# A layer of linear attention in four rounds: the next round's features are made within the heads, and the second norm is spread over the next round

## What is computed

```python
q, k, v = src @ Wq + bq, src @ Wk + bk, src @ Wv + bv      # 16 heads of 64
Q = jax.nn.elu(q) + 1.0
K = jax.nn.elu(k) + 1.0
KV = jnp.einsum('bshd,bshm->bhdm', K, v)
Z = 1.0 / (jnp.einsum('bshd,bhd->bsh', Q, K.sum(axis=1)) + EPS)
o = jnp.einsum('bshd,bhdm,bsh->bshm', Q, KV, Z).reshape(b, s, H * DH)
x = _layer_norm(src + o @ Wo + bo, g1, be1)
y = gelu(x @ W1 + b1) @ W2 + b2
return _layer_norm(x + y, g2, be2)                          # added to x by the caller
```

## Time and profile before

| | us |
|---|---|
| median of 3 runs | 3260.01 (3257.52 to 3273.21) |
| profiled execution, its own time | 3263.29 |
| its span, first to last instruction | 3261.6 |
| mean granted TensorE clock | 0.934 |
| TensorE matmuls busy | 2924.0 (90%) |
| VectorE / ScalarE / GpSimd busy | 1800.6 (55%) / 1350.9 (41%) / 683.8 (21%) |

### The profile page before, as it was taken

How to read it: one execution, slowest core, us unless ns; L and a number is a source line. 1 busy time by engine, 2 the same in 40 slices (tenths; PEclk the granted TensorE clock), 3 DMA queues, 4 the chain that set the end, 5 groups by cost and what they waited for, 6 DMA issues and landing times.

```text
span 3261.6 us, 64530 instructions
## 1 busy us (share of the span) xinstructions
PE 2924.0 (90%) x24081; PEld 1889.0 (58%) x24081; DVE 1800.6 (55%) x5820; ACT 1350.9 (41%) x3669; POOL 683.8 (21%) x1535
## 2 busy tenths in 40 slices
PE   8999988787799996998778997659999999999899
PEld 7888856555457774666445775444444444444465
DVE  6777765656326666756866665762233233333444
ACT  4565552223238882236676885421112111121221
POOL 3444420000017770003304663000000000000000
PEclk9999998988899996987788998979999999999999
DMA  5111100000012110030022113012000000000000
GB/s 129 46 49 46 47 24 1 1 1 1 4 27 53 47 31 22 1 108 4 13 45 59 39 40 136 2 53 76 1 1 1 1 1 1 1 1 1 1 1 14
DMA packets 158813, 91.86 MB, mean 28 GB/s; under 512 B 74211, under 2 KB 155750, under 8 KB 157414
## 3 DMA queue, kind: packets, MB, share of 16 engines
q1 hardware_dynamic: 158502, 87.74, 9.9%
HBM read 84.02 MB, written 3.67 MB: 27 GB/s over the span
## 4 chain that ended last, share of the span: by engine, by line
PE 51%; DVE 7%; issue 5%; POOL 5%; ACT 3%; POOLq 2%; DVEq 1%; ACTq 0%
PE banks L3253 23%; POOL probs L1198 3%; PE banks L3669 2%; PE banks L3660 2%; PE banks L3658 2%; PE banks L1593 2%; POOLq L1199 2%; PE banks L908 2%; PE banks L3314 1%; ACT inner L3036 1%; PE banks L889 1%; PE banks L1831 1%; PE banks L3308 1%; PE banks L2201 1%; PE banks L917 1%
## 5 line engine op out<-in xcount | busy, mean ns | idle before, releaser
L998 ACT ACTIVATE probs<-probs,nbias 128x257 f32<-128x257 f32 x512 | 254.8, 507 | 0.0
L1198 POOL TENSOR_SCALAR probs<-probs,rinv 128x257 f32<-128x257 f32 x512 | 237.9, 485 | 31.6 <-DVE rinv L1092 28.3
L3253 PE MATMUL banks<-Wn,hT 128*64 128x512 f32 x1024 | 226.7, 595 | 0.0
L3253 PE MATMUL banks<-Wz,hT 128*64 128x256 f32 x2048 | 226.4, 379 | 0.0
L3253 PE MATMUL banks<-Wr,hT 128*64 128x512 f32 x1024 | 225.2, 592 | 0.0
L3519 POOL COPY rb<-hT 128x512 f32<-128x512 f32 x32 | 35.8, 1118 | 824.5 <-ACT hT L3326 799.5
L3253 PEld LDWEIGHTS banks<-Wz,hT 128*64 128x64 f32 x2048 | 147.0, 137 | 87.7 <-issue 18.3
L3493 DVE TENSOR_TENSOR pr<-hb,banks 128x512 f32<-128x512 f32 x32 | 22.0, 687 | 298.4 <-PE banks L3308 298.4
L702 POOL TENSOR_SCALAR probs<-probs,rinv 128x257 f32<-128x257 f32 x256 | 120.6, 485 | 204.0 <-DVE rinv L642 203.4
L3253 PEld LDWEIGHTS banks<-Wr,hT 128*64 128x64 f32 x1024 | 73.6, 137 | 132.4 <-issue 127.8
L3253 PEld LDWEIGHTS banks<-Wn,hT 128*64 128x64 f32 x1024 | 70.7, 137 | 132.9 <-issue 129.5
(11 more groups left out here) (631 smaller groups left out, 6744.0 us busy)
## 6 DMA issues: line engine op xcount, KB each, us to landing
kvT<-in_ctx_T SPq DMA_DIRECT2D x192, 128.5 KB
kv<-in_ctx SPq DMA_DIRECT2D x64, 128.0 KB
kv<-in_ctx SPq DMA_DIRECT2D x32, 256.0 KB
W<-in_L_ffn_W SPq DMA_DIRECT2D x64, 64.0 KB, 2.1
Wr<-in_L_ffn_w_hh_T SPq DMA_DIRECT2D x1, 4096.0 KB
Wn<-in_L_ffn_w_hh_T SPq DMA_DIRECT2D x1, 4096.0 KB
Wz<-in_L_ffn_w_hh_T SPq DMA_DIRECT2D x1, 4096.0 KB
v_last<-v_last SPq DMA_DIRECT2D x192, 8.0 KB, 1.6
```

Source lines behind the costliest of these rows:

```text
L998: i = e.activation(s, s, ACT.Exp, bias=self.nbias[v][:, r:r + 1], scale=self.scale, accum_out=self.rows_sum[v][:, r:r + 1])
L1198: e.tensor_scalar(s, s, self.rinv[v][:, r:r + 1], 1.0, ALU.mult, ALU.mult)
L3253: mm = e.matmul(self.bank[b][hf * BATCH:(hf + 1) * BATCH, 0:n], lhs, rhs, start=start, stop=stop, tile_position=(0, hf * BATCH))
```

## The change

`features`, `exp_features` and `make_features` for chunks 0 to 4 of round r+1 are moved into the heads of round r, after units 2 to 6 (`CHUNK_AT`). Chunk 5 comes ahead of the last tile's projection, chunk 6 ahead of the turn of x1, chunk 7 between `hidden` and `outward`. `feat` gets a second pair of tiles for it. To keep banks 0 and 1 for the features, the values share one bank (2) and the projection's transposes, `onto_y` and `outward` share another (3). `project` is split: its first half comes at the start of an even unit, its second half behind that unit's `apply`. The second norm of a round, the sum onto X and the next statistics are cut into seven parts, and part u is done after unit u of the next round (all seven behind one another after round 3). The turn of x1 starts from the normed rows; ScalarE applies g1 and be1 while copying it, and VectorE applies them to s1 only afterwards. The first norm's statistics are taken tile by tile in `add_y`. bo is added to y by GpSimd ahead of use (`y_bo`). Parts 0 to 6 of `second_norm` are: the bias b2; statistics and variance; the root's reciprocal and the rows; times g2; plus be2; X plus s2; the next layer's statistics. The diff, cut to its core (first `pe`, then `act`, then `dve`):

```diff
+    def rows_dve(self, e, src, dst):
...
+    CHUNK_AT = {2: 0, 3: 1, 4: 2, 5: 3, 6: 4}
+    VALUES, TURNS = 2, 3
...
+        self.g1_col, self.be1_col = self.columns("g1_col", w["g1"]), self.columns("be1_col", w["be1"])
-        self.feat = [sb("qf", [P, C * R4]), sb("kf", [P, C * R4])]
+        self.feat = [[sb("qf", [P, C * R4]), sb("kf", [P, C * R4])] for _ in range(2)]
+        self.y_bo = [sb("y_bo", [P, R4]) for _ in range(2)]
...
         for r in range(self.ROUNDS):
+            more = r + 1 < self.ROUNDS
-            self.values(e, r, 0)
+            self.values(e, r, 0, 0)
             self.weights(e, r, 0)
+            self.values(e, r, 0, 1)
             for u in range(8):
                 s, j = u // 2, u % 2
+                if j == 0 and s:
+                    self.project(e, r, s - 1, 0)
                 if u < 7:
                     self.weights(e, r, u + 1)
-                if j == 1 and s < 3:
-                    self.values(e, r, s + 1)
+                if s < 3:
+                    self.values(e, r, s + 1, j)
                 if j == 1 and s:
                     self.onto_y(e, r, s - 1)
                 self.apply(e, r, u)
                 if j == 0 and s:
-                    self.project(e, r, s - 1)
-            self.project(e, r, 3)
+                    self.project(e, r, s - 1, 1)
+                if more and u in self.CHUNK_AT:
+                    self.features(e, r + 1, self.CHUNK_AT[u])
+            if more:
+                self.features(e, r + 1, 5)
+            self.project(e, r, 3, 0)
+            self.project(e, r, 3, 1)
             self.onto_y(e, r, 3)
-            for c in range(self.C):
-                if r + 1 < self.ROUNDS:
-                    self.features(e, r + 1, c)
-                if c == 1:
-                    self.turn_x1(e, r)
-                if c == 2:
-                    self.hidden(e, r)
-                if c == 3:
-                    self.outward(e, r)
+            if more:
+                self.features(e, r + 1, 6)
+            self.turn_x1(e, r)
+            self.hidden(e, r)
+            if more:
+                self.features(e, r + 1, 7)
+            self.outward(e, r)
...
+    def values(self, e, r, s, n):
+        self.values_ready.wait_ge(e, 8 * r + 2 * s + n)
...
+    def project(self, e, r, s, n):
         self.o_ready.wait_ge(e, 16 * r + 4 * s + 4)
+        self.oT_ready.wait_ge(e, 8 * r + 2 * s + n)
+        for q in range(4):
+            i = e.transpose(self.bank[self.TURNS][:, q * P:(q + 1) * P], self.o_tok[s % 2][:, (4 * n + q) * P:(4 * n + q + 1) * P], self.prog.ident[:, :])
+        i.then_inc(self.o_turned.up(), 1)
...
         for r in range(self.ROUNDS):
+            for u in range(8):
+                if u % 2 == 0 and u:
+                    self.take_turned(e, r, u // 2 - 1, 0)
+                    if r and u == 2:
+                        self.norm.act(e)
+                    self.take_turned(e, r, u // 2 - 1, 1)
+                if more and u in self.CHUNK_AT:
+                    self.exp_features(e, r + 1, self.CHUNK_AT[u])
+            if more:
+                self.exp_features(e, r + 1, 5)
+            self.take_turned(e, r, 3, 0)
+            self.take_turned(e, r, 3, 1)
+            if more:
+                self.exp_features(e, r + 1, 6)
+            self.norm.act(e)
...
+            e.activation(self.x1T[:, :], self.bank[self.VALUES][:, :], ACT.Identity, bias=self.be1_col[:, 0:1],
+                         scale=self.g1_col[:, 0:1]).then_inc(self.x1T_ready.up(), 1)
...
+            if more:
+                self.exp_features(e, r + 1, 7)
+        self.norm.act(e)
...
             for u in range(8):
                 s, j = u // 2, u % 2
+                if u < 7:
+                    self.within_batch(e, r, u + 1)
+                if s < 3:
+                    self.add_values(e, r, s + 1, j)
                 if j == 1 and s:
                     self.add_y(e, r, s - 1)
-                if u < 7:
-                    self.within_batch(e, r, u + 1)
+                if more and u - 1 in self.CHUNK_AT:
+                    self.make_features(e, r + 1, self.CHUNK_AT[u - 1])
                 self.over_sums(e, r, u)
+                if r:
+                    self.second_norm(e, r - 1, u)
+            if more:
+                self.make_features(e, r + 1, 5)
             self.add_y(e, r, 3)
+            self.norm.variance_dve(e)
+            self.norm.rows_dve(e, self.s1, self.s1)
+            e.drain().then_inc(self.s1_ready.up(), 1)
+            if more:
+                self.make_features(e, r + 1, 6)
+            else:
+                for q in range(3):
+                    self.next_rows(e, q)
+            self.x1_turned.wait_ge(e, r + 1)
+            e.tensor_tensor(four(self.s1), four(self.s1), row4(self.g1), ALU.mult)
+            e.drain()
+            e.tensor_tensor(four(self.s1), four(self.s1), row4(self.be1), ALU.add)
+            e.drain()
+            if more:
+                self.make_features(e, r + 1, 7)
+            self.w2_mm.wait_ge(e, r + 1)
+            e.tensor_tensor(self.s2[:, :], self.bank[self.TURNS][:, :], self.s1[:, :], ALU.add).then_inc(self.s2_ready.up(), 1)
+            e.drain()
+        for part in range(7):
+            self.second_norm(e, self.ROUNDS - 1, part)
+
+    def second_norm(self, e, r, part):
...
     def add_y(self, e, r, s):
         at = slice(s * P, (s + 1) * P)
-        e.tensor_tensor(self.s1[:, at], self.bank[0][:, 0:P], self.bo[:, :], ALU.add).then_inc(self.bo_added.up(), 1)
+        e.tensor_tensor(self.s1[:, at], self.bank[self.TURNS][:, 0:P], self.y_bo[r % 2][:, at], ALU.add).then_inc(self.bo_added.up(), 1)
         e.drain()
-        e.tensor_tensor(self.s1[:, at], self.s1[:, at], self.prog.y[:, r * R4 + s * P:r * R4 + (s + 1) * P], ALU.add)
+        self.norm.moments_dve(e, self.s1, s)
+        e.drain()
+
+    def pool(self, e):
...
+        for r in range(self.ROUNDS):
+            self.bo_added.wait_ge(e, 4 * (r - 1))
+            e.tensor_tensor(four(self.y_bo[r % 2]), p.y[:, r * R4:(r + 1) * R4].rearrange("p (t d) -> p t d", d=P), row4(self.bo),
+                            ALU.add).then_inc(self.y_bo_ready.up(), 1)
```

More of the change, by code:

```diff
@@ L293, in finish_dve @@
     def finish_dve(self, e, src, dst, gain, offset):
+        self.rows_dve(e, src, dst)
+        e.drain()
+        e.tensor_tensor(four(dst), four(dst), row4(gain), ALU.mult)
+        e.drain()
+        return e.tensor_tensor(four(dst), four(dst), row4(offset), ALU.add)
+    def rows_dve(self, e, src, dst):
         self.std.wait_ge(e, self.var.count)
@@ L299, in finish_dve @@
                             self.rstd[:, u:u + 1], ALU.subtract, ALU.mult)
[L300 to L303, removed]
 class SoftmaxCrossAttention(Stage):
@@ L1329, in features @@
         for t, W in enumerate((self.Wq, self.Wk)):
[L1330 to L1335, removed]
+            self.n_yT.wait_ge(e, 4)
+            self.feature_ready.wait_ge(e, f + t - 1)
             e.matmul(self.bank[t][:, :], W[:, c * P:(c + 1) * P], self.prog.yT[:, r * R4:(r + 1) * R4],
                      start=True, stop=True).then_inc(self.feature_mm.up(), 1)
[L1339 to L1346, removed]
+    def values(self, e, r, s, n):
+        self.values_ready.wait_ge(e, 8 * r + 2 * s + n)
+        self.x1T_ready.wait_ge(e, r)
+        self.n_yT.wait_ge(e, 4)
+        e.matmul(self.bank[self.VALUES][:, :], self.prog.yT[:, r * R4 + s * P:r * R4 + (s + 1) * P],
+                 self.Wv[:, n * 512:(n + 1) * 512], start=True, stop=True).then_inc(self.value_mm.up(), 1)
     def weights(self, e, r, u):
@@ L1386, in onto_y @@
         for c in range(8):
-            i = e.matmul(self.bank[0][:, 0:P], self.oT[s % 2][:, c * P:(c + 1) * P], self.Wo[:, c * P:(c + 1) * P], start=c == 0, stop=c == 7)
+            i = e.matmul(self.bank[self.TURNS][:, 0:P], self.oT[s % 2][:, c * P:(c + 1) * P], self.Wo[:, c * P:(c + 1) * P], start=c == 0, stop=c == 7)
         i.then_inc(self.onto_mm.up(), 1)
@@ new lines, in act, with take_turned @@
+            self.w2_mm.wait_ge(e, r)
+            for k in range(4):
+                self.w1_mm.wait_ge(e, 4 * r + k + 1)
+                e.activation(self.hT[:, k * R4:(k + 1) * R4], self.bank[4 + k][:, :], ACT.Gelu,
+                             bias=self.b1[:, k:k + 1]).then_inc(self.gelu_ready.up(), 1)
+            if more:
+                self.exp_features(e, r + 1, 7)
+        self.norm.act(e)
+    def take_turned(self, e, r, s, n):
+        self.o_turned.wait_ge(e, 8 * r + 2 * s + n + 1)
+        self.onto_mm.wait_ge(e, 4 * r + s - 1)
+        e.copy(self.oT[s % 2][:, n * 512:(n + 1) * 512], self.bank[self.TURNS][:, :]).then_inc(self.oT_ready.up(), 1)
@@ new lines, in dve @@
+            e.drain()
[3 more added lines that the diff above has]
+            e.tensor_tensor(self.s2[:, :], self.bank[self.TURNS][:, :], self.s1[:, :], ALU.add).then_inc(self.s2_ready.up(), 1)
+            e.drain()
+        for part in range(7):
```

(18 more changed lines are left out.)

114 lines of the change are left out of this document (37 added, 77 removed).

## The result

| | before | changed |
|---|---|---|
| median, us | 3258.92 (4 runs) | 3229.47 (4 runs) |
| profiled execution, its own time / span, us | 3263.29 / 3261.6 | 3231.99 / 3230.2 |
| mean granted TensorE clock | 0.934 | 0.941 |

The ratio is 0.9901, 95% interval 0.9873 to 0.9929: faster by 1.0%, some 30 us. The forecast was 39 us less, 3220.6 us; 3229.5 lies in its range of 3203 to 3244, nine us above the forecast itself.

A forecast was written before the change was run, and what follows sets the result against it. Heads were taken as bound by TensorE, tails by a three-engine chain. Heads 52.3, tail 24.2 and clock 4.8 give 81.3 a round against 94.4, 39.4 less over three, round 3 nothing: 3220.6 us, range 3203 to 3244.

The forecast's parts named there:

- the sum: Whole stage: new round 81.3 against 94.4 us, 13.1 less, three times 39.4; round 3 nothing.
- The walk through the heads: Heads of rounds 1 and 2, followed unit by unit at 2.4 GHz: 52.3 us instead of 43.0.
- my allowance for the clock: Heads: 1.9 us for a cold stretch (six in ten) behind unit 2's new 1.4 us wait.
- The reading of what a chunk costs: Heads: five chunks of features take 8.75 us of TensorE and 0.5 us more.
- Tail: End of rounds 0 to 2: chain through the first norm's root, second norm off the path, 24.2 us instead of 49.0.
- The clock's terms: Added per round for 1.2 GHz work: hidden 1.9, onto_y 1.0, heads 1.9; together 4.8 us, bounds 0 and 7.0.
- Round 3: Last round, no chunks: heads 48.2 us with one cold stretch against 46.2, tail 30.3 against 32.3; net 0.
- Rival 4: Second norm's parts on VectorE delay within_batch and the next weights: + 14 us, 3235; chance 0.10.
- Rival 2: Chunks hide badly in the heads, 3.46 us each against 1.87: 24 us come back, 3244; chance 0.13.
- Rival 1: TensorE's clock stays up in heads and tails: 57 us less in all, 3203; chance 0.14.
- Rival 3: Heads fall to 1.2 GHz behind new waits: 138 us in all, 3319, slower from 40% of it; chance 0.05.

The follow-up runs named there:

- e1: Changed kernel, in round 3 only the projection's first half again behind the even unit's apply, second half behind the next weights; ratio 0.9862 to the kernel before, stage 352.5 us.
- e3: Changed kernel with all seven second-norm parts back at the end of their own round; ratio 1.0010 to the kernel before, stage 390.1 us.
- e6: Changed kernel with the first norm's root and x1's copy ahead of chunk 6's exponentials on ScalarE; ratio 0.9877 to the kernel before, stage 349.0 us.
- e8: Changed kernel with g1 and be1 applied by VectorE ahead of the turn again, plain copy on ScalarE; ratio 0.9972 to the kernel before, stage 370.6 us.
- e9: The changed kernel run once more, unaltered (the repeat); 3225.6 against 3255.3 us, ratio 0.9923 to the kernel before, stage 356.0 us.
- e4: Changed kernel with feature chunks 0 to 4 back in the tail ahead of chunk 5; ratio 1.0019 to the kernel before, stage 406.8 us.
- e5: e4 with the projection behind apply in all rounds, as in e2; ratio 0.9958 to the kernel before, stage 363.4 us.
- e2: e1 with the projection behind apply also for unit 2 of rounds 0 to 2; ratio 0.9875 to the kernel before, stage 345.8 us.
- e7: Changed kernel with the edits of e2 and e6 together; median 3197.5 us, ratio 0.9838 to the kernel before, stage 331.8 us.

## Why the prediction was right, and where not

The mechanism stood: with five chunks and the second norm moved, tails of rounds 0 to 2 shrank by 20 to 23 us and heads grew by 7 to 11. The profiles moved by 31.3 us where the sum had 39.4. Of the 8.1 us that are missing, 5.9 are round 3 and 2.2 are rounds 0 to 2 (246.1 against 243.9), in which larger errors cancelled.

**The walk through the heads: right.** Its moments beside the trace of round 1 (counted from the first values, 581.06):

| TensorE begins | walk | trace |
|---|---|---|
| projection of tile 0, first half (the new wait) | 12.5 | 12.7 |
| chunk 0 | 17.4 | 17.5 |
| chunk 1, after a wait for chunk 0 on VectorE | 25.5 | 26.0 |
| projection of tile 1 | 27.45 | 27.9 |
| chunk 2 | 32.4 | 33.0 |
| chunk 3 | 40.5 | 41.6 |
| chunk 4 | 46.8 | 48.0 |
| end of the last apply | 52.3 | 53.5 |

The waits ahead of chunks are 0.96, 0.19, 0.89 and 0.45 us, where I had 0.6, 0.05, 0.6 and 0.35: each wait for VectorE is 0.1 to 0.4 us longer than the durations add up to. Two rows of unit 3 in round 1:

```profile
604.23 1.90 PE L1388 MATMUL banks<-vext,att 128*128 128x65 f32 x16
607.08 1.12 PE L1357 MATMUL banks<-yT,Wq 128*128 128x512 f32 x2 [0.96 <-DVE qf L1564]
```

With my allowance for the clock I had 54.2 a round; the three heads measured 55.0, 53.5 and 53.5, a sum 0.6 less. That is luck. The walk was 1.2 us short in each round, and in round 0 by 1.4 more, a wait of TensorE for the last chunk of its features that it didn't have. The allowance of 1.9 was for a cold stretch behind unit 2's wait, and this profile has none: the errors cancelled. The stretch itself is real. Over the changed kernel, e1, e3, e6, e8 and e9, which have the same order there, it stands in 5 of 18 such halves (e1 and e9 round 2, e8 rounds 0 to 2) and costs 1.6 us; I had given it six in ten, at 3.2.

**The reading of what a chunk costs: near in sum, wrong in its parts.** "Five chunks for 8.75 us of TensorE and 0.5 us more" is 9.3, and round 1's half grew by 10.5. Yet e4 shows that the new order alone costs 9.9 us without a chunk (52.9 against 43.0) and with it the chunks are nearly free, and e5 that without this order they cost 10. The step that missed this is the early projection: I charged its wait where no chunk fills it (1.4 us), and didn't see that elsewhere the heads pay either for the chunks or for the waits and cold work that the order has without them.

**Tail: mechanism right, the waits and one term of the clock too small.** The chain through the root stood as written: chunk 6's exponentials, the table load, the root, then the turn, after a wait of 4.43 us (I had 4.4). ScalarE's rows in the tail of round 0 of the changed kernel:

```profile
562.56 0.69 ACT L1480 ACTIVATE ex<-banks,bq 128x512 f32<-128x512 f32 x1 [4.63 <-PE banks L1357]
563.42 0.69 ACT L1480 ACTIVATE ex<-banks,bk 128x512 f32<-128x512 f32 x1 [0.17 <-PE banks L1357]
564.14 0.66 ACT L1483 ACTIVATE banks<-banks,bk 128x512 f32<-128x512 f32 x1
564.82 1.28 ACT L300 ACT_TABLE_LOAD   x1
566.11 0.21 ACT L300 ACTIVATE rstd<-rstd 128x4 f32<-128x4 f32 x1
```

VectorE had the variance ready by 563.4 (L296 starts at 562.69), so about 2.7 us of the path were chunk 6 and a table load; e6 took them away. The walk gave 24.2 and the clock 2.9, 27.1 a round; measured 29.3, 28.3, 26.6, in sum 2.9 more. Two things make up the difference. `onto_y` begins 6.19 us behind the last apply in each round, where the walk had 5.65: 1.6 us in three rounds, in waits for VectorE and ScalarE. The clock's terms give the rest, and they miss in both directions. The one that was mis-sized is hidden behind the wait: I took + 1.9 from the pair of features at 2.07 us, a chunk of 1.75 that was over before the clock came back; hidden is twice as long and was cold for most of it in rounds 0 and 1, 6.6, 6.8 and 5.2 us instead of 3.7, with the turn ahead of it cold too in rounds 1 and 2 (1.12 us instead of 0.66). For onto_y I took half: it was cold in round 0 (3.67) and warm in rounds 1 and 2 (2.05), 1.6 us instead of 3.0. In the repeat it was cold in rounds 0 and 2 (3.49, 3.52): half of six, as allowed for. By the Trainium skill's rule in "TensorE: Matmul & The Clock Gate" (Part 4: PE-mode transpose), that transposes don't count as busy for the clock, I would have had it cold each round. The two traces of the changed kernel have it cold in 3 of 6 rounds with a chunk ahead, so by them the rule doesn't decide it there.

**Round 3: wrong, + 5.9 instead of 0.** The walk gave heads of 45.0 at full clock and I added one cold stretch of 3.2. I had the three waits of 1.36 us, but only that one stretch. The trace has a cold stretch behind each wait: weights, values, transposes, an apply and an onto_y at 1.2 GHz add 7.8 us to 45.1, so the walk was right and the clock's term was 4.6 short. In the repeat the half came to 48.3, the number of the forecast (48.2) but by another way: no cold stretch at the first wait and shorter ones at the second and third. e1 takes the three waits and their stretches away together and is at 43.5, e2 at 41.9. The tail is 31.5 and 30.5 in the two profiles, forecast 30.3.

**The rest.** Outside the stage the start, 2.6 us later, and the end, 2.5 us shorter, cancel; the medians moved by 29.5 us where the two profiles moved by 31.3. GpSimd's four instructions took 1272 ns each (I had 1163), and nothing waited for them; whether an instruction of VectorE with two SBUF inputs suffers beside them isn't shown, since none ran beside them (the memsets beside the first two, which read nothing, took 0.93 us as before). The table switches of the second norm in unit 2 were covered: round 0, without them, and round 1 take the same 40.8 us from there on. Rival 4 is refuted by this and by e3; its price was also added up for two rounds, while three (1 to 3) have norm parts. Rival 2 is refuted by e5, 2.0 us for a chunk in the heads and not 3.46. Rival 1's clock came true in the heads of rounds 0 to 2 only; e7 shows that it is to be had in two tails too. Rival 3 was true for round 3 alone: 7.8 us in a half at a clock of 0.84. The 3319 us that it names for all of its price took the gain off twice; 3220.6 + 138 is 3359.

What stays open: why the same stretch is cold in one execution and warm in another (round 3's heads 52.9 and 48.3; e8's heads; onto_y in the tails). In round 3 of the changed kernel the clock fell at the wait of unit 2, and in round 1 it stayed up at the same wait behind the same instructions. So the length of a wait and the instructions right around it don't decide it alone. No run set this apart.

## What to carry to other kernels

When work is moved from a loose stretch into a tight one, walk the engines' lists through their waits; the sum of busy times would have given no stall and no order of stalls, and the walk was right within 0.5 us a step. Then ask of each new place in the order what it costs where the filler is missing: here the last round and the first projection of each, 13 us of 359 that e2's condition gave back, a few of them the clock's. And charge a wait of TensorE with the cold work that may follow it as well as with itself: in round 3 the three waits are 4.1 us and the cold work behind them 7.8 in one execution, 3.2 in the other. Such a term is a range, and one profile doesn't give it.

## What the runs showed of the hardware

- The granted clock can fall at a wait of 1.36 us: between an apply (65 columns a matmul) and transposes, the next weights take 2.08 instead of 1.16 us. In round 3, without chunks, it fell at three of three such waits in one profile of the changed kernel and at two of three in the other. In rounds 0 to 2 the one such wait was followed by it in one of six halves (clock 0.97; the other five 1.00), and the waits of 0.9 us ahead of a chunk of 512-column matmuls in none. Whether the shorter wait or the chunk kept it up there was not told apart.
- Transposes run at either level: four take 0.66 us at 2.4 GHz and 1.12 at 1.2.
- A table load can be done ahead of the wait of the instruction that needs it: in e6 ScalarE loads at once behind the copy and then sits 4.04 us until the variance comes.

```profile
555.97 1.28 ACT L300 ACT_TABLE_LOAD   x1
561.29 0.20 ACT L300 ACTIVATE rstd<-rstd 128x4 f32<-128x4 f32 x1 [4.04 <-DVE rstd L296]
```

- It isn't always. For the first gelu of a round in the changed kernel, the load comes ahead of the wait in round 0 (first two rows) and only once the first matmul has landed in rounds 1 to 3 (third row, round 1). In the code the gelu waits for one semaphore more from round 1 on (`w2_mm`); no run tested whether that is the reason.

```profile
569.30 1.28 ACT L1464 ACT_TABLE_LOAD   x1
571.45 0.69 ACT L1464 ACTIVATE hT<-banks,b 128x512 f32<-128x512 f32 x1 [0.86 <-PE banks L1420]
...
653.08 1.28 ACT L1464 ACT_TABLE_LOAD   x1 [2.21 <-PE banks L1420]
```

- Code that is the same in all variants took 2389.6 to 2412.3 us behind the stage, and the stage's start lay between 463.6 and 468.3 us, so a difference of 5 us between two variants can't be read in the totals of two profiles.
